# Second attention: gathers in halves of 64 rows, the following chunk's statistics in a chunk's fourth unit

## The reference

```
x = x + attention0(layernorm(x), ctx)      # softmax(q k^T / 4 + mask) v, then an output projection
x = x + experts(layernorm(x))              # 2 shared + the best 2 of 8 routed experts (1024 hidden units)
x = x + attention1(layernorm(x), ctx)
x = x + sqrt(real^2 + imag^2)              # two 256 x 256 products of layernorm(x), with cos and sin weights
```

## Time and profile before

| | us |
|---|---|
| median of three runs | 1293.83 (1291.77 to 1296.13) |
| profiled execution | 1307.28 |
| its span, first to last instruction | 1305.5 |

### The profile page before, as it was taken

One profiled execution on the slowest core, in us unless ns is written; L12 is line 12 of the kernel. 1 busy time (PEld: TensorE's weight loads), 2 busy tenths in 40 slices (PEclk: granted clock), 3 DMA queues, 4 the chain that ended last, 5 costly groups with the idle time before them and its releaser, 6 DMA issues. The chain is left out here.

```text
span 1305.5 us, 43625 instructions
## 1 busy us (share of the span) xinstructions
PE 1178.0 (90%) x17942; PEld 583.4 (45%) x17942; DVE 677.9 (52%) x1622; ACT 1038.3 (80%) x1482; POOL 174.1 (13%) x211
## 2 busy tenths in 40 slices
PE   8888798898898999999999999977879999998995
PEld 5322232232222356677899988642222223222222
DVE  5325656756646576554666666653235343333335
ACT  3599899999999855443666666539999999999993
POOL 5111111011001030333000010323120000000000
PEclk9999999999999999999999999989999999999997
DMA  6236734534636333211443354222120010010001
GB/s 189 67 115 228 249 105 138 177 105 147 194 108 219 92 116 108 91 64 49 121 139 106 113 153 126 81 71 81 38 60 11 19 29 2 19 28 2 3 3 65
DMA packets 106305, 124.94 MB, mean 96 GB/s; under 512 B 25091, under 2 KB 89310, under 8 KB 106142
## 3 DMA queue, kind: packets, MB, share of 16 engines
q1 hardware_dynamic: 89088, 85.95, 21.5%
q0 software_dynamic: 9328, 29.37, 7.2%
q10 hardware_dynamic: 7726, 7.26, 1.9%
HBM read 70.27 MB, written 46.95 MB: 90 GB/s over the span
## 5 line engine op out<-in xcount | busy, mean ns | idle before, releaser
L888 ACT ACTIVATE prob<-banks 128x1024 f32<-128x1024 f32 (+1 forms) x832 | 772.5, 1048 | 17.8 <-PE banks L1679 14.1
L1694 PE MATMUL banks<-prob,v 64*32 64x512 f32 x6656 | 443.7, 594 | 0.6 <-ACT prob L888 0.6
L1679 PE MATMUL banks<-zone,kst 52*32 52x512 f16 x6528 | 336.7, 384 | 90.4 <-ACT prob L888 82.5
L1679 PEld LDWEIGHTS banks<-zone,kst 52*32 52x32 f16 x6528 | 92.7, 89 | 500.3 <-ACT prob L888 478.4
L1694 PEld LDWEIGHTS banks<-prob,v 64*32 64x32 f32 x6656 | 119.1, 106 | 22.0 <-ACT prob L888 2.4
L2327 PE MATMUL banks<-xsT_d,w 128*128 128x128 f16 x1776 | 123.6, 219 | 3.3 <-DMA w<-weight_parts 1.5
L2327 PEld LDWEIGHTS banks<-xsT_d,w 128*128 128x128 f16 x1776 | 108.7, 98 | 12.3 <-issue 9.2
L2338 PE MATMUL banks<-w,hh 128*128 128x256 f16 x592 | 107.0, 273 | 0.0
L2124 DVE TENSOR_TENSOR hl<-hid,hh 128x128 f16<-128x128 f32 x296 | 83.3, 291 | 31.8 <-ACT hh L2051 23.7
L2047 ACT ACTIVATE hid<-banks,b 128x128 f32<-128x128 f32 x222 | 74.5, 368 | 25.1 <-PE banks L2327 21.0
L2290 PE MATMUL banks<-w,hh 128*128 128x256 f16 x480 | 80.6, 276 | 2.0 <-DVE outb_d L2209 2.0
(11 more groups left out here) (275 smaller groups left out, 1289.0 us busy)
## 6 DMA issues: line engine op xcount, KB each, us to landing
weight_parts<-late SPq DMA_DIRECT2D x54, 256.0 KB, 3.4
w<-weight_parts POOLq DMA_DIRECT2D x24, 512.0 KB, 4.0
late<-in_L_ffn_W_r SPq DMA_DIRECT2D x43, 256.0 KB, 4.2
weight_parts<-more SPq DMA_DIRECT2D x26, 256.0 KB, 3.3
zone<-q_parts SPq DMA_DIRECT2D x180, 32.0 KB
slot_rows<-late POOLq DMA_DIRECT2D x14, 384.0 KB, 4.4
more<-in_L_ffn_W_r SPq DMA_DIRECT2D x21, 256.0 KB, 4.1
xs_d<-slot_rows ACTq DMA_DIRECT2D x39, 128.0 KB, 2.1
```

What stands on the lines that cost most here:

```text
L888: nc.scalar.activation(prob[0:m, t % P_RING, 2 * (n % 2):2 * (n % 2) + 2, :], score[G % S_RING][0:m, :, :], ACT.Exp, scale=0.25).then_inc( ...
L1679: last = nc.tensor.matmul(score[G % S_RING][j:j + wide, a, :], kst[stack, 2 * q + n % 2, t * P + j:t * P + j + wide], qst[stack, u % Q_RIN ...
L1694: last = nc.tensor.matmul(outp[u % 2][GROUP * j:GROUP * (j + 1), a, :], v[rows, t, u % NQ, j, :], prob[rows, (u * KT + t) % P_RING, j, :], ...
```

## The change

Chunks 2 and 3 are gathered by `halved_gather`: each of the eight gathers becomes two, of rows 0 to 63 and of rows 64 to 127, and each waits on POOL until the one before has landed. The upper half takes its row numbers from `slot_low`, a copy of the lower 64 partitions' numbers of `g.slot` that a new transfer on SP makes at the block's start. Chunk 2's gathers stay where they are in POOL's order; `scales` (POOL's share of the layernorm behind the output projection) of chunk 0 goes ahead of chunk 3's. DVE takes the statistics of chunk 2 in unit 3 instead of unit 2, those of chunk 3 in unit 7 instead of units 4 (statistics) and 6 (`normalise`), directly behind `finish`, and ahead of the unit's `take_wave`.

```diff
@@ -382,10 +383,11 @@
-        def gather(pool, into, c, n, signal):
+        def gather(pool, into, c, n, signal, rows=slice(0, P)):
             t, k = c * TPC + n // 2, n % 2
-            pool.indirect_dma_start(out=into[:, n, :], out_offset=None, in_=g.result_dram,
-                                    in_offset=bass.IndirectOffsetOnAxis(ap=g.slot[:, k, t:t + 1], axis=0)).then_inc(signal, 16)
+            pool.indirect_dma_start(out=into[rows, n, :], out_offset=None, in_=g.result_dram,
+                                    in_offset=bass.IndirectOffsetOnAxis(ap=(g.slot_low if rows.start else g.slot)[0:rows.stop - rows.start, k, t:t + 1],
+                                                                        axis=0)).then_inc(signal, 16)
@@ -475,6 +477,8 @@
+            if not first:
+                sp.dma_start(g.slot_low[:], g.slot[HALF:P]).then_inc(low_loaded, 16)
             sp.wait_ge(maskt_ready, 1)
@@ -670,6 +674,15 @@
+            def halved_gather(c, n):
+
+                if c == 2 and n == 0:
+                    pool.wait_ge(low_loaded, 16)
+                for half in range(2):
+                    if n or half:
+                        pool.wait_ge(gathered[c], 16 * (2 * n + half))
+                    gather(pool, home[c], c, n, gathered[c], slice(HALF * half, HALF * (half + 1)))
+
@@ -761,11 +774,12 @@
+                if c >= 1:
+                    scales(c - 1)
                 if not first and 2 <= c + 2 < NC:
                     for n in range(GATHERS):
-                        paced_gather(c + 2, n)
+                        halved_gather(c + 2, n)
                 if c >= 1:
-                    scales(c - 1)
                     if first:
                         split_rows(c - 1)
@@ -1375,8 +1389,6 @@
                         untangle(c + 1, 1)
-                    if done and c + 2 < NC:
-                        query_statistics(c + 2)
                     if done:
                         add_projection(c - 1, 0)
@@ -1394,16 +1406,14 @@
-                    if not done:
-                        query_statistics(c + 2)
-                        normalise(c + 2)
                     if done:
                         take_turned(c - 1, 0)
                         take_turned(c - 1, 1)
                         take_wave(c - 1, 0)
-                    if done and c + 2 < NC:
+                if not first and q == 3:
+                    if c + 2 < NC:
+                        query_statistics(c + 2)
                         normalise(c + 2)
-                if not first and q == 3:
                     if done:
                         for i in range(1, TPC):
                             take_wave(c - 1, i)
```

More of the change, by code:

```diff
@@ L288, in attention @@
             gathered = [None] + [sem(f"gathered{c}") for c in range(1, NC)]
+            low_loaded = sem("low_loaded")
             tile_gathered = [sem(f"tile_gathered{i}") for i in range(TPC)]
@@ L778, in _ @@
                 for c in range(1, NC):
-                    pool.wait_ge(gathered[c], 16 * GATHERS)
+                    pool.wait_ge(gathered[c], 16 * GATHERS * (1 if c == 1 else 2))
         @block.scalar
@@ L955, in query_statistics @@
                 elif c:
-                    combine(c, home[c], gathered[c], GATHERS, added, GATHERS * c)
+                    combine(c, home[c], gathered[c], GATHERS * (1 if c == 1 else 2), added, GATHERS * c)
                 else:
@@ L2422, in program @@
         g.slot = sb("slot", [P, 2, NT], mybir.dt.uint32)
+        g.slot_low = sb("slot_low", [HALF, 2, NT], mybir.dt.uint32)
         g.gate = sb("gate", [P, NT, E_R], F32)
```

## The result

The changed kernel takes 1308.27 us (median of three runs, 1307.59 to 1313.33) against 1293.83: ratio 1.0113, 95% interval 1.0089 to 1.0138, so 14.4 us slower. The forecast was 1299 (1289 to 1312), which is 5.2 us slower: the sign and the range hold, the size does not, and two terms of the sum are wrong by more than the sum. The profiled execution is the 1313.33 one, span 1311.5.

The account below looks back on a forecast made before the run. The prediction took ACT's exponentials to bound the last three quarters of the second attention. Its terms -4.9 + 8.4 + 1.5 + 0.2 summed to +5.2 us, giving a forecast of 1299 us, range 1289 to 1312.

Parts of the forecast that it names:

- Pauses that go: Second attention, units 1 to 4: eight ACT pauses beside the 128-row gathers of chunks 2 and 3 vanish, -4.9 us.
- pauses that come: Second attention: ACT pauses beside the 32 half gathers of chunks 2 and 3, +8.4 us, 4.3 of it beside chunk 3's.
- the price per us of gathering: ACT pauses of 4.93 us over 49.8 us of gathering chunks 2 and 3: 0.099 us per us.
- a rival: No change: halves near 2.4 us with half the pauses, or pauses the profiler causes; 1290 to 1297 us, chance 0.22.
- Half gather: POOL, 64 rows: 0.89 us to issue plus 1.70 us wait, 2.59 us in all, bounds 1.49 and 2.98.
- SyncE's traffic: Chunk 3's half gathers: SyncE's loads stretch them by 1.9 us, as they stretched one whole gather.
- Statistics of chunk 3: Unit 7, DVE: gathers land at 1067.1, 5.8 us late, less 4.3 us of pauses: +1.5 us.
- Chunk 2, and what moved at no cost: Chunk 2's statistics in a later unit, `scales` ahead of chunk 3's gathers, DVE's moved arithmetic: 0 us each.
- `slot_low`: Its new load, first in SyncE's queue ahead of the mask loads, costs 0 to 0.4 us, taken as +0.2.
- the pause does not depend on the rows: Rival: halves take 2.98 us, chunk 3 lands 12.1 us late; +12.1 us, 1306 us, chance 0.19.
- lockstep: Rival: every half issue meets a score group's end, 0.70 us for each of 32; +17.7 us, 1311.5 us, chance 0.13.

Follow-up runs that it names:

- the kernel with early halves: Changed kernel with `scales` of chunk 0 back behind chunk 3's half gathers, so these start right behind chunk 2's bias; 1295.17 us, 0.9997 of the kernel before.
- SyncE's loads held back: Changed kernel with SyncE's loads of chunk 2's queries waiting until chunk 3's last half gather has landed; 1309.74 us, 1.0115 of the kernel before.
- twelve transfers: Changed kernel with only chunk 3's first four gathers in halves and its last four whole; 1296.30 us, 1.0021 of the kernel before.
- the waves first: Changed kernel with chunk 3's statistics and `normalise` behind the three `take_wave` of unit 7 on DVE; 1300.87 us, 1.0039 of the kernel before.

## Why the prediction was right in sign and wrong in its terms

*Pauses that go (-4.9) and pauses that come (+8.4).* Both are wrong, the second by all of it. The step that failed is the price per us of gathering, worked out from the coincidence of pauses and issues in one profiled execution. Two more profiles of the same program show whole gathers without such pauses, the changed kernel shows halves without them (0.54 us in all, where the prediction named less than 3 us as the sign against its rate), and the kernel with early halves runs like before. "Whatever 128-row issues cost is gone" removed nothing. The doubt stood in the text (an execution 1.0% above the median, pauses that "could be smaller"), but it went into a rival, not into the sum.

*Half gather (2.59 us).* The issue, forecast at 0.89, took 0.90. The wait, forecast at 1.70, took mostly 1.77 to 1.93 undisturbed: 2.7 to 2.8 us for a half. Taking half of the moving time of the earlier trace rows off the wait was too much. The estimate of 2.83 us by the Trainium skill's rule (DMA: Bandwidth & Descriptors, Anatomy of one DMA) was nearer; the trace agrees within 0.1 us, and with its point that the cost of such a transfer is nearly all fixed (half of the rows saved 0.23 of 2.98 us).

*SyncE's traffic (+1.9).* The mis-sized term. Sixteen undisturbed halves of 2.75 us make 44.0, and the stretch took 53.4 and 50.1 us: 6 to 9 us of stretching. The bound was carried over from chunk 3's old place as one collision, put down to SyncE's loads; that gather (962.04 to 966.92) had 271 packets of SyncE's and a fetch of the program beside it. A stretch twice as long meets several, and most of the excess (7.7 of 9.2 us in the first profile) lies in waits with a fetch, which the term did not know of.

*Statistics of chunk 3.* The mechanism, the unit and the deadline hold. The window from the first half to the deadline was forecast as 1061.3 - 1023.8 = 37.5 us and is 1048.44 - 1010.87 = 37.6. The landing was forecast 43.3 us after the first half and came after 53.4, so 15.8 us late instead of 5.8; then 4.3 us of pauses, which did not exist, were taken off to leave 1.5. Four executions follow one line, lateness against pauses: 0.3 and 0.17, 11.1 and 13.07 (SyncE's loads held back; 11.61, 1.11 and 0.35 us), 12.65 and 14.29, 15.8 and 17.87. What is above one to one, 1.6 to 2.1 us, comes with the stops only: PE's lower clock behind them, a term that the sum lacked.

*Chunk 2, and what moved at no cost.* The prices are right. Chunk 2's last half was issued at 949.63; DVE waited 3.13 us for it, until 952.28, but ACT has no pause there. That the hour agrees with the forecast (about 952) is luck: the halves took 49 us instead of 41.4 and started 7 us earlier. `scales` ahead of the gathers waited for DVE's `ovar`, as forecast. Moved statistics with whole gathers take 0.9990 of before.

*`slot_low` (+0.2).* From the end of the experts' last store on SyncE to the first exponential it was 42.63 us (832.59 to 875.22) and is 42.79 (826.20 to 868.99), with the load of 0.56 us between. But the changed kernel's second profile has 42.38 (826.64 to 869.02) and the unchanged kernel's two others 42.65 and 42.71, so no run shows a cost of this load. SyncE's queue of the changed kernel, beside the earlier trace rows:

```profile
829.43 0.56 SPq L481 DMA_DIRECT2D slot_low<-slot  x1
```

*The sum.* In place of -4.9 + 8.4 + 1.5 + 0.2 stand 0 + 0 + 14.3 to 17.9 + 0, which the timed 14.4 and 14.0 (1308.50 - 1294.54) meet at the lower end. Had the first term been left at nothing and no pauses been credited in unit 7, the same steps would have given 5.8 + 0.2: still too little, by the size of the stretch. Of the rivals, "the pause does not depend on the rows" gave 1306 by a landing 12.1 us late, which is about what happened, with pauses that did not. So it is partly luck that sign and range hold: 3.5 of the forecast's 5.2 us came from pauses that are not there, and the upper part of the range, where the result lies, was there for that rival and for "lockstep", and neither rival's pauses occurred. What was foreseen is that a late landing in unit 7 costs time, and why.

## What to carry to other kernels

A stall that appears in one profiled execution is priced only after a second profile of the same program, above all where that execution is longer than the median. A series of transfers that each wait for the one before costs its number of round trips, so cutting transfers smaller lengthens it almost in proportion (16 halves take 44 us undisturbed, 8 whole ones 24); compare its landing with the moment from which the in-order engine behind it holds up the bound engine, and leave room for several collisions on the way. Where the landing can't be earlier, it is the consumer's place in the order that decides. Two transfers per wait, or an earlier start, took the whole loss away here; the waves first on DVE left about 5 us of it.

## What the runs showed of the hardware

An indirect transfer of 64 rows took 0.90 us to issue on POOL and about 1.85 more until the next could be issued, one of 128 rows 0.94 and about 2.04. Two halves issued back to back landed in the wait of one (1.77 to 1.83 us).

Fetches of the program ran beside such transfers: 16 KB each (0.11 MB in seven packets), about every 7 us here. In the shown stretch the half beside one took 3.6 us and the next 2.4, and none of the 99 waits without one was longer than 2.41 us. The Trainium skill (Runtime: NRT & Kernel Launch, Instruction fetch mechanics) tells that programs are refilled in blocks of 16 KiB and calls the cost mostly hidden; the size agrees. That sentence is on a program's own step from block to block; how long a transfer beside a fetch takes it does not say. That the fetch is the cause of the longer waits rests on coincidence in time; no run took it away.

PE's granted clock falls in a stop, and the work behind it pays: 16 matmuls on the values took 1.93 us there instead of 1.04. With the waves first PE stopped for only 3.06 us (until 1075.42), and its windows (columns as above) read:

```profile
1068.00:1072.60 4.60, 3.69 (x88) 1.02 (x72) 3.31 (x13) 4.60 (x7) 1.04 (x1) 1.00 0.00 0
1072.60:1077.00 4.40, 1.58 (x20) 1.08 (x28) 4.25 (x9) 0.94 (x2) 2.35 (x1) 0.71 0.02 4
1077.00:1080.00 3.00, 3.00 (x48) 0.76 (x40) 2.86 (x5) 1.76 (x2) 0.00 (x0) 0.50 0.00 0
1080.00:1084.00 4.00, 3.93 (x76) 1.28 (x68) 1.50 (x3) 3.50 (x5) 0.00 (x0) 0.84 0.00 0
```

The tail is a second wait of ACT of 1.11 us, the same in all four executions with such a stop (3 to 16 us). With twelve transfers, where ACT paused for 0.17 us, the clock stayed at 1.00.
